# LN2's statistics taken one slot earlier than its subtraction, magnitude and scales

## The reference

```
x = x + attention(layernorm(x), ctx, ctx, mask)      # 16 heads of 32, 120 keys
x = x + bitlinear(gelu(bitlinear(layernorm(x), w1, b1)), w2, b2)
layernorm(x) = (x - mean(x)) / sqrt(var(x) + 1e-5)
bitlinear(x, w, b) = act_quant(rmsnorm(x)) @ weight_quant(w).T + b
act_quant(x): scale = 127 / max|x| of the row; round(x * scale) / scale
weight_quant(w): scale = 1 / mean|w|; clip(round(w * scale), -1, 1) / scale
```

## Time and profile before

| | |
|---|---|
| median of 3 runs | 765.94 us (760.66 to 766.47) |
| profiled execution | 764.71 us, span 762.9 us |
| granted TensorE clock, mean | 0.968 |
| PE busy | 666.9 us, 87% |
| DVE busy | 604.4 us, 79% |
| ACT busy | 521.7 us, 68% |
| POOL busy | 505.8 us, 66% |

### The profile page before, as it was taken

One profiled execution on the slowest core, in us unless ns is written; L12 is line 12 of the kernel. 1 busy time (PEld: TensorE's weight loads), 2 busy tenths in 40 slices (PEclk: granted clock), 3 DMA queues, 4 the chain that ended last, 5 costly groups with the idle time before them and its releaser, 6 DMA issues.

```text
span 762.9 us, 13877 instructions
## 1 busy us (share of the span) xinstructions
PE 666.9 (87%) x4856; PEld 428.1 (56%) x4856; DVE 604.4 (79%) x1060; ACT 521.7 (68%) x1455; POOL 505.8 (66%) x645
## 2 busy tenths in 40 slices
PE   7756778989999999999999999999999998887885
PEld 5434566656666556556655666656655664554432
DVE  3396776789788897889887978889788778888783
ACT  2254544797578778877687767877888878777360
POOL 3056343776867777777777687767777768777664
PEclk9978889999999999999999999999999999999998
DMA  9933012043322421243334332252223233232244
GB/s 308 378 123 125 12 37 69 22 104 76 76 49 57 125 51 53 64 118 76 76 63 118 76 77 57 55 122 57 54 52 74 66 63 63 63 63 64 56 77 110
DMA packets 109204, 65.37 MB, mean 86 GB/s; under 512 B 90775, under 2 KB 90775, under 8 KB 108495
## 3 DMA queue, kind: packets, MB, share of 16 engines
q1 hardware_dynamic: 108079, 64.49, 33.8%
q10 hardware_dynamic: 1056, 0.00, 0.1%
HBM read 35.12 MB, written 8.39 MB: 57 GB/s over the span
## 4 chain that ended last, share of the span: by engine, by line
PE 36%; DVE 35%; ACT 16%; issue 5%; DMA 4%; POOL 3%; SPq 1%; ACTq 0%; DVEq 0%; POOLq 0%
PE ps_a L405 13%; PE ps_z L507 5%; DVE hid L870 5%; DVE yw L854 5%; ACT prob L693 5%; PE ps_y L522 4%; PE ps_a L435 4%; PE ps_a L478 3%; ACT hid L700 3%; DVE yq L857 2%; PE ps_t L466 2%; DVE bn L849 2%; DVE nmax L834 2%; DVE ps_s L831 2%; DVE oT_l L799 2%
## 5 line engine op out<-in xcount | busy, mean ns | idle before, releaser
L1106 POOL TENSOR_TENSOR prob<-prob,pinv 128x480 f32<-128x480 f32 x128 | 126.3, 987 | 177.5 <-DVE pinv L839 177.5
L693 ACT ACTIVATE prob<-ps_s,nmax 128x120 f32<-128x120 f32 x512 | 180.2, 385 | 34.5 <-DVE nmax L834 34.1
L507 PE MATMUL ps_z<-w1T,q_xT 128*128 128x512 bf16 x476 | 123.9, 383 | 5.6 <-DMA q_xT<-q_x 4.5
L870 DVE SCALAR_TENSOR_TENSOR hid<-ps_z,y_deq,b_row 128x512 f32<-128x512 f32 x119 | 88.6, 744 | 45.3 <-PE ps_z L507 45.3
L693 ACT ACTIVATION_READ_ACCUMULATOR prob<-ps_s,nmax 128x1 f32 x512 | 118.2, 231 | 0.0
L522 PE MATMUL ps_y<-w2T,q_hT 128*128 128x512 bf16 x480 | 114.1, 382 | 0.3 <-DMA q_hT<-xn 0.3
L831 DVE COPY_PREDICATED_SCALAR ps_s<-hidden_key,masked_c 128x480 f32 x128 | 89.5, 700 | 16.4 <-PE ps_s L456 16.4
L466 PE MATMUL ps_t<-ident,prob 128*120 128x128 f32 x512 | 79.2, 278 | 18.0 <-ACT probT L665 10.9
L834 DVE TENSOR_REDUCE nmax<-ps_s 128x4 f32<-128x480 f32 x128 | 84.1, 657 | 4.4
L665 ACT COPY probT<-ps_t 120x512 f32<-120x512 f32 x128 | 79.5, 621 | 7.6 <-PE ps_t L466 7.2
L466 PEld LDWEIGHTS ps_t<-ident,prob 128*120 128x120 f32 x512 | 59.8, 139 | 40.4 <-ACT probT L665 21.3
(11 more groups left out here) (155 smaller groups left out, 1397.6 us busy)
## 6 DMA issues: line engine op xcount, KB each, us to landing
xn<-in_x_dram SPq DMA_DIRECT2D x8, 1024.0 KB, 5.7
x<-in_x_dram SPq DMA_DIRECT2D x32, 256.0 KB, 2.7
out_dram<-x SPq DMA_DIRECT2D x32, 256.0 KB, 3.2
hid<-in_L_ffn_w_dram SPq DMA_DIRECT2D x4, 1024.0 KB, 8.8
w2T<-in_L_ffn_w_dram SPq DMA_DIRECT2D x2, 1024.0 KB, 14.0
ctx_k<-in_ctx_dram SPq DMA_DIRECT2D x8, 240.0 KB, 4.0
ctx_k<-in_mask_Bx1xSxS_ik_dram SPq DMA_DIRECT2D x7, 240.0 KB, 2.8
wk_s<-in_L_xattn_wk_dram SPq DMA_DIRECT2D x1, 1024.0 KB, 8.6
```

The source lines that it names most:

```text
L507: last = nc.tensor.matmul(bank[:], q_xT[:, k % 3, i], w1T[:, i, c * CH:(c + 1) * CH], start=(i == 0), stop=(i == KD - 1))
L693: last = nc.scalar.activation(prob[:, n % 3, g * S2:(g + 1) * S2], ps_s[n % HG][:, g * S2:(g + 1) * S2], ACT.Exp, bias=nmax[:, n % 4, g:g ...
L870: v.scalar_tensor_tensor(hid[:, k % 2, c * CH:(c + 1) * CH], z_bank(FC * k + c)[:], y_deq[:, k % 8:k % 8 + 1], b1_row[:, c * CH:(c + 1) * ...
L1106: gp.tensor_tensor(pr, pr, pinv[:, n % 4].unsqueeze(2).to_broadcast([P, HG, S2]), ALU.mult).then_inc(s["prob_ready"], 1)
```

## The change

The function `ln2_scales` is cut in two. `ln2_stats` holds bn_stats and bn_aggr and runs in the slot of the residual (LN20 = 10), at the end of DVE's slot, behind the magnitude of h. `ln2_scales` keeps the rest and stays in its slot (SC20 = 11). In the tail behind the last slot the two are called one behind the other, as before.

```
-    ... RES0, LN20, RX0, B20 = ... 10, 11, 12, 13
+    ... RES0, LN20, SC20, RX0, B20 = ... 10, 10, 11, 12, 13
...
-            def ln2_scales(k):
+            def ln2_stats(k):
                 t = k % T
                 wait(dve, "x2_ready", k + 1)
                 v.bn_stats(out=bn2[:, t], in_=x2[:, x2_at(k)]).then_inc(s["ln2_part"], 1)
                 wait(dve, "ln2_part", k + 1)
                 v.bn_aggr(out=mv2[:, t], in_=bn2[:, t]).then_inc(s["ln2_stats"], 1)
+
+            def ln2_scales(k):
+                t = k % T
                 wait(dve, "ln2_stats", k + 1)
                 wait(dve, "qx_ready", k - 1)
                 v.tensor_scalar(yw[:, k % 2], x2[:, x2_at(k)], mv2[:, t, 0:1], None, ALU.subtract
...
                     h_scale(k)
                 k = tile_at(n, LN20)
                 if k is not None:
+                    ln2_stats(k)
+                k = tile_at(n, SC20)
+                if k is not None:
                     ln2_scales(k)
...
+            ln2_stats(30)
             ln2_scales(30)
...
+            ln2_stats(31)
             ln2_scales(31)
```

More of the change, by code:

```diff
@@ L51, in xattn_bitffn_kernel @@
     LAG = 3
-    LOAD0, BO0, ATT0, LOW0, WO0, RES0, LN20, RX0, B20 = 2, 6, 7, 8, 9, 10, 11, 12, 13
+    LOAD0, BO0, ATT0, LOW0, WO0, RES0, LN20, SC20, RX0, B20 = 2, 6, 7, 8, 9, 10, 10, 11, 12, 13
     UP0, GELU0, SQ0, ABS0, QH0, HF0, DOWN0, YOUT0 = 14, 17, 18, 18, 19, 21, 22, 24
```

## The result

The changed kernel takes 741.96 us (median of 4 runs, 739.78 to 742.45), the kernel before 766.21 beside it: a ratio of 0.9685, 95% interval 0.9644 to 0.9725. The sign was right and the size wrong. Of all runs in this document one, of the kernel with a short delay (754.47 us, mean granted clock 0.956), is in the chip's slower state and is left out of that kernel's figures.

The account below looks back on a forecast made before the run. No single engine bounded the kernel (PE 36%, DVE 35% of the chain), and Pool's phase set the subtraction's end. Terms -8.4 - 0.6 - 1.4 - 1.3 - 0.5 + 4.0 = -8.2 us gave 757.7 us, range 750 to 769.

Parts of the forecast that it names:

- Slot 11: n mod 16 = 11, tiles 4 to 24: subtraction ends 1.99 us earlier, PE gains; -1.4 x 6 = -8.4 us.
- Slot 7: Tiles 3 to 27, k mod 4 = 3: late pinv, subtraction misses the rounding boundary; +0.57 x 7 = +4.0 us.
- The third rival: Pool's second rounding goes first at the boundary though DVE waited; +13, 779 us; chance 0.11.
- the fourth: Move only shifts time between two DVE slots, 0.94 and 0.82 us cancel; 765 us; chance 0.22 with the first.
- the first: Transposes of q_x become the wall in slot 14; about +1, 766.9 us, range 762 to 769; 0.22 with the fourth.
- No subtraction of LN2 now waits so: At the rounding boundary: no present case, so the weight stage's L928 showed DVE goes first; second rounding some 0.2 us longer.
- the term of slot 15: Tiles 5, 9, 17, 21: PE gain capped at 1.26 us, nearly all given back to late q_xT; -0.35 x 4 = -1.4.
- Slot 3: Tiles 6, 18, 22: subtraction ends near 488.15 against 488.30, nothing; tiles 10 and 26: -1.3 and -0.5 us.
- the -1.3 for tile 10: Subtraction of tile 10, k mod 4 = 2: in the slow phase now; -1.3 us, from the 1.26 us cap.
- The last batch: Tiles 26 to 29: -0.5 for tile 26, +0.6 for 27, -0.6 for 28, 0 for 29.
- The second rival: q_xT lands faster than 4.28 us, so no wall in slot 2; -15.3, 750.6 us; chance 0.17.

Follow-up runs that it names:

- the kernel with a short delay: Changed kernel plus one unused 384-column tensor_reduce on DVE between evac_up and the subtraction, some 0.47 us per tile; 744.66 us, ratio 0.9716.
- early_slot7: Kernel before, with statistics taken a slot earlier only for tiles with k mod 4 = 3; 768.28 us, ratio 1.0041.
- before_accum: Kernel before, statistics unmoved, with the subtraction also writing the row's sum, a form that takes no shared port; 749.93 us, ratio 0.9799.
- turn_first: Changed kernel with SP's transpose of q_x put ahead of the store of the same slot; 741.61 us, ratio 0.9704.
- the pair without the port: Kernel before and changed kernel, each with the subtraction also writing the row's sum, which takes no shared port; 749.93 and 732.98 us.

## Why the prediction was wrong

**Right.** The mechanism: the subtraction goes in between Pool's two roundings and ends 0.29 us behind the first (0.28 forecast). Slot 11: -1.4 forecast for each tile, -1.4 measured at tiles 8 to 24. Slot 7: +0.57 forecast, +0.5 to +0.7 measured at five of the first six tiles, +0.2 at tile 15 (+0.65 there in early_slot7); early_slot7 gives +3.9 in all. The third rival (Pool first at the boundary) and the fourth (nothing but a shift within DVE) didn't happen; the first (transposes of q_x as the wall in slot 14) neither.

**Right with a wrong reading.** "No subtraction of LN2 now waits so" is false; tile 31's did:

```profile
722.32 1.97 POOL L1113 TENSOR_SCALAR hid<-hid,hs 128x2048 f32<-128x2048 f32 x1 [0.82 <-DVE hs L883]
...
723.88 0.69 DVE L854 TENSOR_SCALAR yw<-x,mv 128x512 f32<-128x512 f32 x1
724.38 1.94 POOL L1120 TENSOR_SCALAR q_h<-hid 128x2048 bf16<-128x2048 f32 x1
```

It ended 0.28 us behind the first rounding, and the second took 1.94 us. The trace of before thus had both answers, who goes first and the 0.04 us that Pool pays for it, without the weight stage.

**Wrong, by steps.** The step that failed first is the term of slot 15, and with it the adding up of slots read one by one.
- "nearly the whole gain given back. With the same queue and a somewhat later need I keep -0.35 x 4", for slot 15. It measured -1.67 each, 5.3 us more in all. I had taken the transfer of 4.28 us behind tile 13 as the rule. The transfers behind the tiles in the sum, 5, 9, 17 and 21, took 2.41 to 2.43 us in the trace that I read, and in the changed kernel they had landed within the 3.2 us before PE's need. The cap was too low as well: I had set it at the one wait for the evacuated x (1.26). In before_accum, where the statistics stay and only the subtraction is short, these distances give 1.25, just that wait; the 0.4 beyond it come with the statistics' move. By what wait, I haven't isolated.
- "Slot 3 ...: nothing", and the sum of separate terms. Slot 3 shows 1.2 + 2.0 + 2.0 + 3.1 = 8.3 for the 1.8 forecast. Of these 1.6 at tile 10 and 0.5 at tile 14 come without slots 15 and 3 changed, and some 1.6 at tile 26 are the clock; so the change's own part is near 4.6 us (an estimate), and the -1.3 for tile 10, whose slow phase I took for a standing one, met its number by luck. The class's worth lay in what it prevents: alone it gives 1.8, but with slot 15 early 11.6 more than slot 15 does alone (13.7 - 2.1). I had taken each slot's phase against Pool from the old timeline, while the change of the slot ahead moves it by 0.3 us.
- The clock, which I left out of the sum: two stretches at half clock less, some 3 us: one less at tile 4 (1.5 of slot 11's -9.8), two less in the last batch, one more at tile 2.
- The last batch (tiles 26 to 29): -5.0 for the -0.5 forecast. Some 3 of it are its two stretches at half clock; turn_first, which has both, shows -2.1 there. What the remaining 2 us come from isn't settled.
- The second rival (750.6) had the right answer on the transfer and was still 9 us short, for the other reasons.

The load of DVE behind evac_up, which the sum used only to place the subtraction, has a worth of its own: 17 us in the pair without the port, some of it the clock's. The move alone gives 24 us, the form without the port alone 16, both together 33: some 7 us are common to the two, and the 24 can't be split into a port's part and a load's part.

## What to carry to other kernels

Where two engines share a port that one of them takes for a whole instruction, the end of the short instruction is set by the phase of the long one: cost it by where it starts, expect steps, and look for a form that doesn't take the port. When such an instruction repeats in several slots of a pipeline, the terms of single slots don't add up, since each shift moves the next slot's phase; test classes in pairs, and widen the range of a sum accordingly. A slow transfer behind one tile is no wall for the others: look at the landings behind the tiles that stand in the sum first. And where an instruction starts within some hundredths of a us of the boundary, as at tiles 10 and 18, one trace can't say which side it falls on: look for the same slot in a second trace.

## What the runs showed of the hardware that I hadn't expected

- A subtraction that begins during Pool's first rounding and has to wait always gets in ahead of the second (156 of 156 in the traces of the kernels with the plain subtraction), though the second begins only 0.09 us behind the first. One that starts at the boundary itself falls either way: 0.49 us at tile 18 before, 2.22 at tile 10, both 2.01 to 2.02 us behind the first rounding's start.
- A subtraction that waits during Pool's first rounding costs the second 0.04 us (1.94 for 1.90); one that starts just ahead of the second, not having waited, costs it 0.2 (2.12 in the earlier trace rows). It had been these that I priced it by.
- The plain subtraction takes 0.48 us where it has the port, the form with the row's sum 0.74 us and 0.08 for reading the sum, everywhere; by the mean (1.22 us) and more by the worst (2.03) the slower form is the faster one.
- The runs of one kernel spread by 3 to 10 us (760.2 to 769.5 in 25 runs of the kernel before). In the profiled ones there are 0 to 7 stretches at half clock, at some 1.5 us each; they can be a part of this, which isn't shown.
